# One step of a state-space layer's pipeline: dt written by ScalarE with its bias, POOL's u, PE's input projection and some of VectorE's small sums one place earlier

## The reference

```
xz = xn @ in_proj_w.T + in_proj_b;  x_in, z = split(xz)
x_conv = silu(causal_conv4(x_in) + conv_b)
Bm, Cm = split(x_conv @ x_proj_w.T + x_proj_b)
delta = clip(softplus(x_conv @ dt_proj_w.T + dt_proj_b), 1e-4, 10)
h[t] = exp(clip(delta*A, -10, 0)) * h[t-1] + delta * Bm * x_conv      # 16 states for each of 512 channels
h = h * min(1, 10/|h|)  at every 16th t
y = sum_n C*h + D*x_conv;  y = y * silu(z);  out = y @ out_proj_w.T + out_proj_b
```

## Time and profile before

| | us |
|---|---|
| median of 3 runs | 4515.41 (4514.4 to 4516.36) |
| the profiled execution | 4514.84 |
| its span, first to last instruction | 4512.8 |
| busy in the span: PE / DVE / ACT / POOL | 4253.3 / 3632.4 / 3057.9 / 2588.5 |
| 1000 to 2000 us, busy: PE / DVE / ACT / POOL | 967.0 / 924.7 / 886.1 / 889.8 |
| 3000 to 4512 us, busy: PE / DVE / ACT / POOL | 1433.2 / 940.7 / 476.7 / 0 |

### The profile page before, as it was taken

One profiled execution on the slowest core, in us unless ns is written; L12 is line 12 of the kernel. 1 busy time (PEld: TensorE's weight loads), 2 busy tenths in 40 slices (PEclk: granted clock), 3 DMA queues, 4 the chain that ended last, 5 costly groups with the idle time before them and its releaser, 6 DMA issues.

```text
span 4512.8 us, 79944 instructions
## 1 busy us (share of the span) xinstructions
PE 4253.3 (94%) x22592; PEld 2960.7 (66%) x22592; DVE 3632.4 (80%) x9610; ACT 3057.9 (68%) x8912; POOL 2588.5 (57%) x1284
## 2 busy tenths in 40 slices
PE   5899999999999999999999999988999999999999
PEld 4777777777777777777777777644444444444444
DVE  3899999999999999999999999855656657566666
ACT  5898888888888888888888888834333332333321
POOL 3988888888888888888888888930000000000000
PEclk8999999999999999999999999999999999999999
DMA  2111111111111111111111111100000000000000
GB/s 101 58 51 62 49 58 53 57 54 57 54 57 54 57 54 57 54 57 54 56 53 54 54 56 55 55 30 22 6 16 16 6 16 6 16 16 7 6 7 10
DMA packets 91560, 187.49 MB, mean 42 GB/s; under 512 B 16160, under 2 KB 58016, under 8 KB 90912
## 3 DMA queue, kind: packets, MB, share of 16 engines
q1 hardware_dynamic: 90272, 180.78, 12.2%
q10 hardware_dynamic: 1152, 5.14, 0.3%
HBM read 168.05 MB, written 17.83 MB: 41 GB/s over the span
## 4 chain that ended last, share of the span: by engine, by line
PE 49%; issue 19%; DVE 18%; POOL 11%; ACT 2%; DVEq 1%; POOLq 0%; DMA 0%; SPq 0%; ACTq 0%
PE ps L684 24%; POOL prod L331 6%; DVE macc L1004 6%; PE ps L658 4%; PE ps L808 3%; POOL hb L339 3%; PE ps L736 2%; PE ps L730 2%; PE ps L750 2%; PE ps L773 2%; PE ps L790 2%; POOL xcv L355 1%; DVE dtt L1189 1%; PE ps_dA L808 1%; PE ps L758 1%
## 5 line engine op out<-in xcount | busy, mean ns | idle before, releaser
L684 PE MATMUL ps<-w_x,mxT 128*128 128x512 f32 x4096 | 1933.7, 601 | 69.6 <-DVE macc L1004 69.6
L1004 DVE SCALAR_TENSOR_TENSOR macc<-ps,gate,macc 128x256 f32<-128x256 f32 x2048 | 977.6, 477 | 498.0 <-PE ps L684 410.0
L915 DVE TENSOR_TENSOR_SCAN hb<-ps_dA,hb 128x1088 f32<-128x1088 f32 x512 | 1240.7, 2423 | 107.4 <-POOL hb L339 99.1
L331 POOL TENSOR_TENSOR prod<-hb,cbc 128x1024 f32<-128x1024 f32 x512 | 1123.1, 2194 | 248.9 <-DVE hb L934 243.5
L339 POOL TENSOR_TENSOR hb<-u,bbc 128x1024 f32<-128x1024 f32 x512 | 1202.0, 2348 | 75.1 <-POOL prod L331 70.9
L394 ACT ACTIVATE zr<-dt,aneg 128x128 f32<-128x128 f32 x4096 | 1240.8, 388 | 1.3 <-DVE dt L1078 1.0
L684 PEld LDWEIGHTS ps<-w_x,mxT 128*128 128x128 f32 x4096 | 727.5, 191 | 739.3 <-issue 604.0
L658 PEld LDWEIGHTS ps<-prod,ident 128*128 128x128 f32 x8192 | 947.5, 192 | 151.9 <-POOL prod L331 91.4
L658 PE MATMUL ps<-prod,ident 128*128 128x128 f32 x8192 | 965.4, 276 | 41.0 <-POOL prod L331 41.0
L403 ACT ACTIVATE ps_dA<-zr 128x1024 f32<-128x1024 f32 x512 | 518.3, 1012 | 0.0
L410 ACT ACTIVATE sq<-hb 128x64 f32<-128x64 f32 x512 | 157.9, 308 | 219.9 <-DVE hb L915 217.4
(11 more groups left out here) (193 smaller groups left out, 4848.3 us busy)
## 6 DMA issues: line engine op xcount, KB each, us to landing
bbc<-bcd SPq DMA_DIRECT2D x128, 512.0 KB, 3.8
cbc<-bcd SPq DMA_DIRECT2D x128, 512.0 KB, 3.7
xt<-in_x SPq DMA_DIRECT2D x128, 128.0 KB, 3.6
x2d<-macc SPq DMA_DIRECT2D x64, 128.0 KB, 1.7
out_dram<-macc SPq DMA_DIRECT2D x64, 128.0 KB, 1.7
w_x<-in_w_x ACTq DMA_DIRECT2D x1, 4096.0 KB, 12.6
hb<-x2d SPq DMA_DIRECT2D x32, 128.0 KB, 2.4
sz<-x2d SPq DMA_DIRECT2D x16, 128.0 KB, 2.2
```

What stands on the lines that cost most here:

```text
L331: TT(dst, states, cc, ALU.mult).then_inc(M["prodp"], 1)
L684: last = mm(banks[p % len(banks)][:], mxT[k][:, j, :], w_x[:, j, p * 512:(p + 1) * 512], start=(j == 0), stop=(j == KD - 1))
L915: V.tensor_tensor_scan(states, dA, states, 0.0, ALU.mult, ALU.add).then_inc(M["scan"], 1)
L1004: STT(macc[k][:], banks[(e // 2) % len(banks)][:, (e % 2) * D:(e % 2 + 1) * D], gate[k][:, e:e + 1], macc[k][:], ALU.mult, ALU.add).then_i ...
```

## The change

- dt: DVE's step in c7 no longer adds the bias. It bounds the projection from both sides by two new columns `dt_hi`, `dt_lo` (the clip's bounds, carried back through softplus and less the bias). ACT's Exp gets the bias, and so becomes four instructions of 128 columns in place of one of 512. Its Ln writes `dt` itself. DVE's clip in c0 (L1078) is gone, and with it the semaphore `dt`; its waiters wait for `ldt`. Ln now also waits for POOL's `u` of the tile before.
- POOL makes `u` in c0 in place of c1, behind `inputs` of chunk 1.
- PE transposes `xn` in c0 ahead of the state sums and does the first half of the input projection in c1; ACT's copy `xnT` moves from c1 to c0.
- DVE: in c0 the residual part stands between BN_STATS and BN_AGGR; in c1 and c3 the sum of squares comes ahead of yg and of the router's maximum.
- DVE's set-up of `dcw` and `ddp` becomes 16 + 4 instructions of 128 columns in place of two broadcast ones, and two instructions for `dt_hi` and `dt_lo` are added.

```diff
@@ POOL @@
             def extra(i, k, c, stages):
-                if c == 1 and "G" in stages:
-                    g.wait_ge(M["dt"], AHEAD + i + 2)
+                if c == 0 and "G" in stages:
+                    g.wait_ge(M["ldt"], AHEAD + i + 2)
                     g.wait_ge(M["xcv"], AHEAD + i + 2)
                     TT(u[1 - k][:], dt[:], xcv[1 - k][:], ALU.mult).then_inc(M["u"], 1)
@@ ACT @@
                 if lo == 0:
-                    a.wait_ge(M["dt"], AHEAD + i + 1)
+                    a.wait_ge(M["ldt"], AHEAD + i + 1)
...
+                    if c == 0 and F:
+                        a.wait_ge(M["xnT"], AHEAD + i + 3)
+                        a.wait_ge(M["z"], AHEAD + i + 2)
+                        for j in range(KD):
+                            act(xnT[:, j, :], F0[:, j * P:(j + 1) * P], ACT.Identity, bias=be_in[:, j:j + 1],
+                                scale=ga_in[:, j:j + 1]).then_inc(M["xnTs"], 1)
                     if c == 1:
...
-                            a.wait_ge(M["xnT"], AHEAD + i + 3)
-                            a.wait_ge(M["z"], AHEAD + i + 2)
-                            for j in range(KD):
-                                act(xnT[:, j, :], F0[:, j * P:(j + 1) * P], ACT.Identity, bias=be_in[:, j:j + 1],
-                                    scale=ga_in[:, j:j + 1]).then_inc(M["xnTs"], 1)
...
                             a.wait_ge(M["dtb"], AHEAD + (i + 3) * EB)
-                            act(dtt[:], dtt[:], ACT.Exp).then_inc(M["edt"], 1)
+                            for e in range(EB):
+                                last = act(dtt[:, e, :], dtt[:, e, :], ACT.Exp, bias=b_dt[:, e:e + 1])
+                            last.then_inc(M["edt"], 1)
                             a.wait_ge(M["edt"], AHEAD + i + 3)
-                            act(dtt[:], dtt[:], ACT.Ln, bias=1.0).then_inc(M["ldt"], 1)
+                            a.wait_ge(M["u"], AHEAD + (i + 2 if G_ else 0))
+                            act(dt[:], dtt[:], ACT.Ln, bias=1.0).then_inc(M["ldt"], 1)
@@ DVE @@
-                if G_:
-                    v.wait_ge(M["ldt"], AHEAD + i + 2)
-                    v.wait_ge(M["zr"], AHEAD + i + 1)
-                    v.wait_ge(M["u"], AHEAD + i + 1)
-                    TS(dt[:], dtt[:], 1e-4, 10.0, ALU.max, ALU.min).then_inc(M["dt"], 1)
...
-                    v.wait_ge(M["dt"], AHEAD + (i + 2 if G_ else 0))
+                    v.wait_ge(M["ldt"], AHEAD + (i + 2 if G_ else 0))
                     for e in range(EB):
-                        TS(dtt[:, e, :], F0[:, e * P:(e + 1) * P], b_dt[:, e:e + 1], 40.0, ALU.add, ALU.min)\
+                        TS(dtt[:, e, :], F0[:, e * P:(e + 1) * P], dt_hi[:, e:e + 1], dt_lo[:, e:e + 1], ALU.min, ALU.max)\
                             .then_inc(M["dtb"], 1)
...
             for dst, w in ((dcw, cw[:].rearrange("p e t -> p (e t)")), (ddp, dpar[:])):
-                n = dst.shape[1]
-                TT(dst[:], ident[:].rearrange("p (a c) -> p a c", a=1).broadcast_to([P, n, P]),
-                   w.rearrange("p (a c) -> p a c", c=1).broadcast_to([P, n, P]), ALU.mult).then_inc(s_zero, 1)
+                for m in range(dst.shape[1]):
+                    last = TS(dst[:, m, :], ident[:], w[:, m:m + 1], None, ALU.mult)
+                last.then_inc(s_zero, 1)
+            for bound_of, x in ((dt_hi, 10.0), (dt_lo, 1e-4)):
+                TS(bound_of[:], b_dt[:], -1.0, math.log(math.expm1(x)), ALU.mult, ALU.add)
```

More of the change, by code:

```diff
@@ L86, in build @@
         dt = sb("dt", [P, EB, P])
+        dt_hi, dt_lo = (sb(n, [P, EB]) for n in ("dt_hi", "dt_lo"))
         dtt = sb("dtt", [P, EB, P])
@@ L156, in build @@
         s_settle, s_passed = sig("s_settle"), sig("s_passed")
-        dve_m = ("st1", "mv1", "vp", "den", "sx1", "nx", "keep", "xib", "zb", "xcc", "bcv", "dtb", "dt", "scan", "nr",
+        dve_m = ("st1", "mv1", "vp", "den", "sx1", "nx", "keep", "xib", "zb", "xcc", "bcv", "dtb", "scan", "nr",
                  "st0", "hs", "yg", "o1", "o2", "st3", "mv3", "vc3", "se3", "r3", "o3", "o4")
@@ L713, in step @@
                         transposes(c - 1)
+                    if c == 0 and F:
+                        pe.wait_ge(M["xn"], AHEAD + i + 3)
+                        pe.wait_ge(M["dtb"], AHEAD + (i + 2) * EB)
+                        for j in range(KD):
+                            last = nc.tensor.transpose(F0[:, j * P:(j + 1) * P], xn[:, j * P:(j + 1) * P], ident[:])
+                        last.then_inc(M["xnT"], 1)
                     if c == 0 and B:
@@ L716, in step @@
                     if c == 1:
-                        if F:
-                            pe.wait_ge(M["xn"], AHEAD + i + 3)
-                            pe.wait_ge(M["dtb"], AHEAD + (i + 2) * EB)
-                            for j in range(KD):
-                                last = nc.tensor.transpose(F0[:, j * P:(j + 1) * P], xn[:, j * P:(j + 1) * P], ident[:])
-                            last.then_inc(M["xnT"], 1)
                         if X_:
@@ L725, in step @@
                             route(i - 2, k, F1)
-                    if c == 2:
-                        if B:
-                            pe.wait_ge(M["yg"], AHEAD + i)
-                            for e in range(EB):
-                                last = mm(YP[:, 0:D], yg[:, e, :], w_out[:, e, :], start=(e == 0), stop=(e == EB - 1))
-                            last.then_inc(M["op"], 1)
                         if F:
@@ L738, in step @@
                             last.then_inc(M["xi"], 1)
+                    if c == 2:
+                        if B:
+                            pe.wait_ge(M["yg"], AHEAD + i)
+                            for e in range(EB):
+                                last = mm(YP[:, 0:D], yg[:, e, :], w_out[:, e, :], start=(e == 0), stop=(e == EB - 1))
+                            last.then_inc(M["op"], 1)
                         if X_:
@@ L934, in bound, with route_norm0, route_norm1 @@
                 STT(last, factor, 1.0, last, ALU.min, ALU.mult).then_inc(M["hs"], 1)
-            def route_norm1(n, x):
+            def route_norm0(n, x):
                 V.bn_stats(mst[:], x).then_inc(R["st"], 1)
+            def route_norm1(n):
                 v.wait_ge(R["st"], AHEAD + n + 1)
@@ L943, in route_norm1, with route_logits, route_scores @@
                 TS(ms[:, 13:14], mmv[:, 0:1], -1.0, None, ALU.mult).then_inc(R["nmm"], 1)
-            def route_scores(n, k, bank):
+            def route_logits(n, bank):
                 v.wait_ge(R["lg"], AHEAD + n + 1)
                 TT(lgt[:], bank[:, D:D + X], rb_row[:], ALU.add).then_inc(R["lgb"], 1)
+            def route_scores(n):
                 v.wait_ge(R["lgb"], AHEAD + n + 1)
@@ L1072, in step @@
                     v.wait_ge(M["x1"], AHEAD + i - 1)
-                    route_norm1(i - 2, x1b[k][:])
-                if G_:
-                    v.wait_ge(M["ldt"], AHEAD + i + 2)
-                    v.wait_ge(M["zr"], AHEAD + i + 1)
-                    v.wait_ge(M["u"], AHEAD + i + 1)
-                    TS(dt[:], dtt[:], 1e-4, 10.0, ALU.max, ALU.min).then_inc(M["dt"], 1)
+                    route_norm0(i - 2, x1b[k][:])
                 if B:
@@ L1082, in step @@
                     STT(oo[:], xt[1][:], r1b[1 - k][:], ob_row[:], ALU.mult, ALU.add).then_inc(M["o1"], 1)
+                if X_:
+                    route_norm1(i - 2)
                 end(0)
                 start(1)
+                halfway(1)
                 if B:
@@ L1091, in step @@
                        sz[1 - k][:].rearrange("p e (h t) -> p h e t", h=4), ALU.mult).then_inc(M["yg"], 1)
-                halfway(1)
                 end(1)
@@ L1111, in step @@
                 if X_:
-                    route_scores(i - 2, k, F1)
+                    route_logits(i - 2, F1)
                 halfway(3)
+                if X_:
+                    route_scores(i - 2)
                 if B:
@@ L1308, in slot @@
                         v.wait_ge(A["x3"], AHEAD + r + 1)
-                        route_norm1(r + NTILES, x3_rows(r))
+                        route_norm0(r + NTILES, x3_rows(r))
+                        route_norm1(r + NTILES)
                     if p == 5:
-                        route_scores(r + NTILES, r % 2, M0)
+                        route_logits(r + NTILES, M0)
+                        route_scores(r + NTILES)
                     if p >= 6:
```

## The result

| | before | after |
|---|---|---|
| median of the runs, us | 4515.48 (4514.4 to 4516.36) | 4543.15 (4539.69 to 4546.25) |
| ratio to before, with its interval | 1 | 1.0064 [1.0052, 1.0076] |
| the profiled execution, us | 4514.84 | 4546.25 |
| its span, us | 4512.8 | 4544.2 |
| granted TensorE clock over the span | 0.987 | 0.978 |

The changed kernel is slower by 0.6 %, 28 us. The forecast was 4462 (4430 to 4506): the time lies outside the range and on the other side.

What follows compares the result with a forecast made beforehand. POOL and DVE were taken to pace the tile in turns, with PE's 44.0 of 45.5 us as floor. 0.81 + 0.15 less 0.05 gives 0.9 a tile, 56 us over 62 tiles, less 2 for set-up: 4462, range 4430 to 4506.

Steps and rivals of the forecast that it cites:

- The 1.27 us fit the 1.28 us of idling: POOL in c0: u, 1.27 us long, would fill the 1.28 us in which POOL idled for DVE.
- Whether it still stays resident at the new place no row tells: ACT's moved, longer loop: may load instructions; one load costs from nothing to about 2 us; not in the sum.
- u in c0, 0.81 a tile: Moving POOL's u to c0 removes all 0.81 us of DVE's idling before the scan of c3.
- dt without DVE's clip and DVE's order, "nearly nothing": DVE between scans of c0 and c2: saves 1.0 to 1.2 us, covered by POOL's inputs, so nearly nothing.
- ACT and `mxn`: ACT in c0: mxn ends about 1531.9, before 1530.79; PE gives back 0.7 us waiting, which doesn't set the end.
- rival B: Gain half eaten on ACT and PE by late mxn or one load a pass: 4480 to 4497; chance 0.18.
- c7: Four Exps cost ACT 0.6 us more in c7, hidden; c4 to c7 stay as they are, shifted.
- c2: PE's wait for `macc`: PE's wait of 0.90 us in c2 for DVE's late expert sums would go.
- Set-up: Separate instructions in place of broadcast ones delay PE's first work by 0 to 3 us once; taken as 2.
- Rival C: Slower: ACT's loop needs two loads a pass, 3.6 us or more; 4542, up to 4590; chance 0.08.
- Rival A: PE becomes the pace at once, all else hidden: 44.0 us a tile, 93 us less, 4422; chance 0.10.
- D: No change: idle before c3 not u's doing, or xn in c0 delays PE's state sums; 4510 to 4520; chance 0.06.

Runs made afterwards that it cites:

- e6_before_u_in_c0: The kernel before with one edit, POOL's u moved to c0; 4499.68 us, 0.9969 of before.
- e1_act_place: The changed kernel with 50 empty semaphore increments on ACT ahead of its loop, which then covers three packets in place of four; 4504.92 us, 0.9981 of before.
- e9: The changed kernel with PE's transposes of xn back in c1 and ACT's copy xnT behind mxn in c1; 4489.24 us, 0.9944 of before.
- e10: The changed kernel with eight identity products, their result overwritten, on PE ahead of its wait for xn in steps with k = 0; 4506.58 us, 0.9981 of before.
- e3_oo_back: e1_act_place with DVE's residual part oo put back behind BN_AGGR and the negation; 4491.24 us, 0.9947 of before.

## Why the prediction was wrong

Two steps failed. The first is "The 1.27 us fit the 1.28 us of idling": from it 0.81 us a tile were taken in full, as if nothing else used POOL's gap. Without the loads the tiles got 0.31 us (even) and 0.26 (odd) shorter for the 0.9 of the sum. The second is the price of ACT's branch, which the sum puts at nothing ("Whether it still stays resident at the new place no row tells"). It came to about 42 us and turned a small gain into a loss. Point by point:

- *u in c0, 0.81 a tile.* On POOL the times came out as forecast where `u` had the ports (4.70 and 5.97 us after the scan). The gap in c2 went in e6_before_u_in_c0, by 0.84. It came back in c1 as 0.58, so `u` alone is worth 15 us. In the order of the change, without the loads (e1_act_place), the distance from the scan of c2 to that of c3 is 5.54 and 5.50 us, for 5.1 forecast and 5.91 before, and c4 takes 0.40 more, which c5 and c6 give back; what holds c2 and c4 there was not followed up. I had looked at the gap as one engine's idle time; the other engine's two-input instruction used it.
- *dt without DVE's clip and DVE's order, "nearly nothing".* The clip's absence lets `u` start without waiting. Putting `oo` ahead of the average was costed only by the 0.15 us of settling that it fills and by ACT's router part starting "about 0.3 later"; that part starts 0.8 to 0.9 later, since `oo` ends with POOL's instruction and `mmv` stands behind. It costs 14 to 17 us.
- *ACT and `mxn`.* "mxn ends at about 1531.9" is 8.6 us after the scan; it was 8.9 to 9.05, for 7.5 before. "waits up to 0.7": without the loads PE waits 1.2 us behind `mxn` in every tile (L673 in e1_act_place, 13.0 us in 11 times and 12.9 in 11 more that the profile puts down to "issue"). "this doesn't set the end" was wrong: with `oo` late, those waits fall to 0.3 to 0.4 and the time by 14 us. It was nearer to rival B.
- *c7.* DVE's bounds from both sides with two columns take 401 ns each for the 341 of before, 4 * 0.06 = 0.24 us a tile that I hadn't counted; c7 got 0.07 to 0.12 longer.
- *c2: PE's wait for `macc`.* Gone, as forecast. *Set-up.* DVE's instructions for `dcw`, `ddp` and the two bounds take 4.2 us, and ACT's first wait for DVE grew from 4.92 to 6.61, 1.7 us for the 2 taken.
- *The loads.* Rival C placed them rightly and named the sign that would show (more than 100 packets; there were 211). Its price was two loads in a chain, 3.6 us or more on the ring. In fact ACT stops for 1.9 to 2.2 us, little of which counts by itself (nothing in e9, 7 to 8 us in before and in e10). What it costs is that PE stands still for it and then runs at 0.50 of its clock, 34 us of it the clock's by the four returns told of above. Rival C's 4542 lies beside the measured 4543 by luck: it takes 4 us a pass on the ring, which no run shows. Nothing in the sum asked what an engine's stall does to PE's clock, because in before PE never stands still for more than 0.92 us from 400 to 2780 us. The chance of 0.08 for it was too low: in how many packets the loop would lie could have been counted, and the text says "no row tells" instead.
- *Rival A* (4422) stays out of reach in all runs; *D* had its reason half right: `xn` ahead of the state sums did hold PE up, when ACT had to load.

The balance, from medians: 4515 before; `u`, clip and the new order with resident code bring it to 4491 (e3_oo_back, about 4 us of padding included); `oo` ahead of the average, + 14, 4505 (e1_act_place); the loads with PE standing still, + 42 less the 4 of padding, 4543.
